# Gate and up products in three ranges of 375, 500 and 375 nodes, codes divided to match, and the feed-forward handed over by bank

## The reference, cut to what matters

```python
def act_qdq(x):                       # one scale for the whole array
    qmax = 2.0 ** (ACT_BITS - 1) - 1.0            # 32767
    scale = jnp.maximum(jnp.max(jnp.abs(x)) / qmax, 1e-12)
    return jnp.clip(jnp.round(x / scale), -qmax - 1.0, qmax) * scale
...
x = act_qdq(x)                                    # 1250 x 1024
up = act_qdq(x @ lpbq_dequant(w_up).T)            # 1250 x 384
gate = act_qdq(x @ lpbq_dequant(w_gate).T)
sig = fixed_qdq_u16(jax.nn.sigmoid(gate))
gate = act_qdq(gate * sig)
o = act_qdq(gate * up)
return o @ lpbq_dequant(w_down).T                 # 1250 x 1024
```

## Time and profile before

| what | us |
|---|---|
| median of 3 executions (1218.94 to 1221.99) | 1220.37 |
| the profiled execution | 1219.83 |
| its span, first to last instruction | 1218.0 |
| feed-forward products on PE, from 1074.17 to 1155.48 | 81.3 |
| handover, PE idle, 1155.48 to 1172.10 | 16.6 |
| down product on PE, from 1172.10 | 41.0 |

### The profile page before, as it was taken

The page is one execution under the profiler, slowest core; times in us unless marked ns, Lnnn a source line. Parts: engine busy times, 40 slices in busy tenths (PEclk is TensorE's granted clock), DMA queues, the critical chain, the costliest instruction groups (busy, mean ns, idle before and its releaser), DMA issues.

```text
span 1218.0 us, 15074 instructions
## 1 busy us (share of the span) xinstructions
PE 1150.2 (94%) x6232; PEld 617.6 (51%) x6232; DVE 680.2 (56%) x1225; ACT 355.0 (29%) x441; POOL 389.7 (32%) x224
## 2 busy tenths in 40 slices
PE   2998899999999999999999999999999999969958
PEld 2554455555555554444444555444444445559823
DVE  7769678656373584238434245746564355672663
ACT  5433333333333233322421122313110012253430
POOL 1267566768787675578100000000000000000000
PEclk9899899999999999999999999999999999989979
DMA  8843653352433437723730134323220080000014
GB/s 258 321 121 54 175 146 83 57 109 20 91 52 58 109 71 226 211 37 118 266 106 1 60 115 153 115 87 110 85 82 18 19 154 1 1 1 1 1 35 134
DMA packets 155997, 117.61 MB, mean 97 GB/s; under 512 B 93372, under 2 KB 132540, under 8 KB 154904
## 3 DMA queue, kind: packets, MB, share of 16 engines
q1 hardware_dynamic: 86616, 103.44, 27.0%
q0 software_dynamic: 69024, 13.07, 8.2%
q10 hardware_dynamic: 288, 0.13, 0.0%
HBM read 90.13 MB, written 21.41 MB: 92 GB/s over the span
## 4 chain that ended last, share of the span: by engine, by line
PE 88%; DVE 6%; issue 2%; ACT 2%; DMA 1%; POOL 0%; SPq 0%; POOLq 0%; ACTq 0%; DVEq 0%
PE ps L1011 34%; PE ps L943 27%; PE ps L1071 7%; PE ps L1043 7%; PE ps L1096 6%; PE ps L1116 3%; PE ps L930 2%; DVE key_b L1198 1%; DMA raw<-in_L_gnn_W_self_dram 1%; DVE whl L1180 1%; PE ps L1059 1%; PE ps L907 1%; PE ps L951 0%; DVE xnT L1186 0%; DVE T L1274 0%
## 5 line engine op out<-in xcount | busy, mean ns | idle before, releaser
L576 POOL DMA_INDIRECT at_scratch<-copies,cell x160 | 342.0, 2137 | 170.8 <-DMA at_scratch<-copies,cell 94.5
L943 PE MATMUL ps<-xnT,whl 128*128 128x512 f16 (+1 forms) x2160 | 385.8, 342 | 4.3 <-DVE T L1278 4.3
L943 PEld LDWEIGHTS ps<-xnT,whl 128*128 128x128 f16 x2160 | 211.8, 99 | 176.0 <-issue 8.9
L1011 PE MATMUL ps<-hb,hT 128*128 128x512 f16 x960 | 207.7, 379 | 1.3 <-DVE hT L1455 1.3
L1011 PEld LDWEIGHTS ps<-hb,hT 128*128 128x128 f16 x960 | 94.0, 98 | 114.4 <-DVE hT L1455 1.8
L1011 PE MATMUL ps<-hb,VT 128*128 128x512 f16 x480 | 103.9, 379 | 1.5 <-ACT S_b L718 1.5
L557 POOL PARTITION_ALL_REDUCE ag_fw<-am_fw x9 | 3.2, 355 | 317.0 <-DVE am_fw L1335 317.0
L1011 PE MATMUL ps<-hb,xnT 128*128 128x512 f16 x480 | 104.2, 379 | 0.0
L1071 PE MATMUL ps<-P,AT 125*128 125x512 f16 x400 | 87.8, 379 | 0.0
L1043 PE MATMUL ps<-AT,P 125*128 125x512 f16 (+1 forms) x480 | 84.7, 339 | 0.0
L1011 PEld LDWEIGHTS ps<-hb,VT 128*128 128x128 f16 x480 | 46.9, 98 | 58.0 <-ACT S_b L718 1.9
(11 more groups left out here) (218 smaller groups left out, 1164.0 us busy)
## 6 DMA issues: line engine op xcount, KB each, us to landing
raw<-in_L_gnn_W_neigh_dram SPq DMA_DIRECT2D x32, 512.0 KB
raw<-in_L_gnn_W_self_dram SPq DMA_DIRECT2D x24, 512.0 KB
key_b<-key_scratch SPq DMA_DIRECT2D x8, 1250.0 KB, 11.4
raw<-in_L_mix_Wo_dram SPq DMA_DIRECT2D x16, 512.0 KB
parts<-at_scratch POOLq DMA_DIRECT2D x20, 312.5 KB, 3.8
at_scratch<-zeros POOLq DMA_DIRECT2D x6, 1020.0 KB, 17.8
x_all<-in_x_dram SPq DMA_DIRECT2D x9, 512.0 KB
x_acc<-in_x_dram SPq DMA_DIRECT2D x9, 512.0 KB, 7.8
```

Of the source, the lines that this page charges most:

```text
L576: pool.indirect_dma_start(out=at_scr[c % 2][:, :], out_offset=bass.IndirectOffsetOnAxis(ap=cell[:, c:c + 1], axis=0), in_=copies[:, c:c + ...
L943: mm = pe.matmul(acc_of(c)[:, a:b], whl[:, i, wp, k, :], xnT[:, k, ap, a:b], start=(k == 0 and wp == 0 and ap == 0), stop=(k == KC - 1 and ...
L1011: mm = pe.matmul(half_bank(i), stationary[:, k, ap, t * TP:t * TP + P], hb[:, n % 2, k, wp, :], start=(k == 0 and wp == 0 and ap == 0), st ...
```

## The change

Five edits, all behind time 1066:

1. `FCOLS` becomes three ranges of 375, 500 and 375 nodes: six products of 72 matmuls each, with 375 or 500 columns, in place of ten with 250.
2. `PIECES` follows: range 0 is coded in pieces of 2, 3 and 3 feature chunks by 375 nodes, then come 250, 250, 250 and 125 nodes by 8 chunks. `CODED` says how many pieces a range needs. The last piece (tile 9 alone) comes on ACT behind `ug_out(0)`.
3. The up products 4 and 5 are copied out and their maxima taken behind the whole gate chain. The last product signals by bank (`ug_bank`), ACT copies bank by bank (`u_part`) and DVE takes each bank's maximum.
4. `TMP` and `TMP2` are computed by ACT, behind its rounding of `U` (`o_times`). The first chunk of `U` is cut at node 500 (`UPARTS`): DVE rounds 500 nodes itself, ACT the rest.
5. Nodes 0 to 124 of `o` are coded in two pieces, chunk 0 and chunks 1 and 2 (`OPIECES`), and PE starts the down product on the first.

```diff
-    FCOLS = [(a, a + 2 * TP) for a in range(0, N, 2 * TP)]
+    FCOLS = [(0, 3 * TP), (3 * TP, 7 * TP), (7 * TP, N)]
...
-    PIECES = [(0, 0, KC // 2), (0, KC // 2, KC)] + [(r, 0, KC) for r in range(1, NR_F)]
+    PIECES = [(0, 3 * TP, 0, 2), (0, 3 * TP, 2, 5), (0, 3 * TP, 5, KC)] + [
+        (a * TP, b * TP, 0, KC) for a, b in ((3, 5), (5, 7), (7, 9), (9, NT))]
+    CODED = [3, 5, 7]
...
+    OPIECES = [(0, 1, 0, TP), (1, IC, 0, TP)] + [(0, IC, a, b) for a, b in OCOLS[1:]]
+    OFIRST = 2
+    UPARTS = [slice(0, 4 * TP), slice(4 * TP, N)] + [slice(c * N, (c + 1) * N) for c in range(1, IC)]
...
+            for n in range(len(PIECES) - 1):
+                code_high(n)
+            turned_x2(NT - 1)
             act.wait_ge(s_ug_ok, 1)
-            for n in range(NR_F):
+            ug_out(0)
+            code_high(len(PIECES) - 1)
+            for n in range(1, NR_F):
                 ug_out(n)
...
+                    if n + 1 == len(UG):
+                        act.wait_ge(ug_bank, b + 1)
...
+            act.activation(sv[:, TMP2:TMP2 + 1], sv[:, Q_GS:Q_GS + 1], ACT.Copy,
+                           scale=sv[:, Q_U:Q_U + 1]).then_inc(o_times, 1)
...
-                    pe.wait_ge(c_lo, r + 2)
+                    pe.wait_ge(c_lo, CODED[r])
...
-                pe.wait_ge(o_lo, r + 1)
+                if r > 0:
+                    pe.wait_ge(o_lo, OFIRST + r)
...
+                            if i == 0 and k < OFIRST:
+                                pe.wait_ge(o_lo, k + 1)
...
-            ug_max(2 * NR_F - 2)
-            steps(ug_max(2 * NR_F - 1))
+            for n in range(NR_F, 2 * NR_F - 1):
+                ug_max(n)
+            for b in range(IC):
+                lo, hi = FCOLS[NR_F - 1]
+                dve.wait_ge(u_part, b + 1)
+                last = dve.tensor_reduce(omax[:, 0, IC * (NR_F - 1) + b:IC * (NR_F - 1) + b + 1],
+                                         U[:, b * N + lo:b * N + hi], AX.X, ALU.max, apply_absolute_value=True)
...
-            steps(dve.tensor_scalar(sv[:, TMP:TMP + 1], sv[:, Q_GS:Q_GS + 1], sv[:, Q_U:Q_U + 1], 1 / 65536.0,
-                                    ALU.mult, ALU.mult))
-            steps(dve.tensor_scalar(sv[:, TMP2:TMP2 + 1], sv[:, TMP:TMP + 1], 1 / 32767.0, None, ALU.mult))
```

More of the change, by code:

```diff
@@ L844, in _ @@
                     turned_x2(t)
[L847 to L851, removed]
             def ug_out(n):
@@ L877, in _ @@
                                scale=65536.0).then_inc(sig_ok, 1)
-                ug_out(NR_F + c)
+                if c == 1:
+                    ug_out(NR_F)
             act.wait_ge(gs_step, 1)
@@ L881, in _ @@
                 round_code(G[:, cols(c)], Q_GS, gs_round)
-            ug_out(2 * NR_F - 2)
-            ug_out(2 * NR_F - 1)
+            for n in range(NR_F + 1, 2 * NR_F):
+                ug_out(n)
             act.wait_ge(u_step, 1)
-            for c in range(1, IC):
-                round_code(U[:, cols(c)], Q_U, u_round)
+            for part in UPARTS[1:]:
+                round_code(U[:, part], Q_U, u_round)
+            act.activation(sv[:, TMP2:TMP2 + 1], sv[:, Q_GS:Q_GS + 1], ACT.Copy,
+                           scale=sv[:, Q_U:Q_U + 1]).then_inc(o_times, 1)
+            act.wait_ge(o_times, 1)
+            act.activation(sv[:, TMP:TMP + 1], sv[:, TMP2:TMP2 + 1], ACT.Copy, scale=1 / 65536.0).then_inc(o_times, 1)
+            act.wait_ge(o_times, 2)
+            act.activation(sv[:, TMP2:TMP2 + 1], sv[:, TMP:TMP + 1], ACT.Copy, scale=1 / 32767.0).then_inc(o_times, 1)
             act.wait_ge(o_step, 1)
-            for r, (a, b) in enumerate(OCOLS):
-                if r == 0:
-                    act.wait_ge(o_code, 1)
-                else:
[L892 to L895, removed]
+            for n, (k0, k1, a, b) in enumerate(OPIECES):
+                if n < OFIRST:
+                    act.wait_ge(o_code, n + 1)
+                else:
+                    act.activation(chunks(G)[:, k0:k1, a:b], chunks(G)[:, k0:k1, a:b], ACT.Identity,
+                                   bias=pos_magic[:, :], scale=sv[:, Q_O + 1:Q_O + 2]).then_inc(o_round, 1)
+                    act.wait_ge(o_round, n - OFIRST + 1)
+                act.activation(o16[:, k0:k1, 0, a:b], chunks(G)[:, k0:k1, a:b], ACT.Identity,
                                bias=neg_magic[:, :]).then_inc(o_hi, 1)
@@ L1092, in _ @@
                     for k in range(KC):
-                        if n == 0 and b == 0 and k % (KC // 2) == 0:
-                            pe.wait_ge(c_lo, k // (KC // 2) + 1)
+                        if n == 0 and b == 0 and k in FIRST_CODED:
+                            pe.wait_ge(c_lo, FIRST_CODED.index(k) + 1)
                         for wp, ap in ((0, 0), (0, 1), (1, 0)):
@@ L1619, in _ @@
                 steps(dve.tensor_scalar(G[:, cols(c)], G[:, cols(c)], MAGIC, None, ALU.subtract))
-            ug_max(2 * NR_F - 2)
-            steps(ug_max(2 * NR_F - 1))
-            code_step(MU, omax[:, 0, :], Q_U, 1.0, u_step)
-            steps(dve.tensor_scalar(sv[:, TMP:TMP + 1], sv[:, Q_GS:Q_GS + 1], sv[:, Q_U:Q_U + 1], 1 / 65536.0,
-                                    ALU.mult, ALU.mult))
-            steps(dve.tensor_scalar(sv[:, TMP2:TMP2 + 1], sv[:, TMP:TMP + 1], 1 / 32767.0, None, ALU.mult))
[L1626 to L1632, removed]
+            for n in range(NR_F, 2 * NR_F - 1):
[5 more added lines that the diff above has]
+                                         U[:, b * N + lo:b * N + hi], AX.X, ALU.max, apply_absolute_value=True)
+            steps(last)
+            code_step(MU, omax[:, 0, :], Q_U, 1.0, u_step)
+            for n, part in enumerate(UPARTS):
+                if n > 0:
+                    dve.wait_ge(u_round, n)
+                code(U[:, part], Q_U, rounded=n > 0)
+                steps(dve.scalar_tensor_tensor(G[:, part], U[:, part], MAGIC, G[:, part], ALU.subtract, ALU.mult))
+                last = dve.tensor_reduce(omax[:, 2, n:n + 1], G[:, part], AX.X, ALU.max, apply_absolute_value=True)
             steps(last)
-            whole_max(MO, omax[:, 2, 0:IC])
+            whole_max(MO, omax[:, 2, 0:len(UPARTS)])
+            dve.wait_ge(o_times, 3)
             steps(dve.tensor_scalar(sv[:, Q_O:Q_O + 1], ag[:, MO:MO + 1], sv[:, TMP2:TMP2 + 1], 1e-12,
@@ L1640, in _, with o_low @@
             dve.wait_ge(o_step, 1)
[L1642 to L1650, removed]
+            def o_low(n):
+                k0, k1, a, b = OPIECES[n]
+                dve.wait_ge(o_hi, n + 1)
+                dve.scalar_tensor_tensor(o16[:, k0:k1, 1, a:b], chunks(G)[:, k0:k1, a:b], MAGIC,
+                                         o16[:, k0:k1, 0, a:b], ALU.subtract, ALU.subtract).then_inc(o_lo, 1)
+            for k0, k1, a, b in OPIECES[:OFIRST]:
+                dve.tensor_scalar(chunks(G)[:, k0:k1, a:b], chunks(G)[:, k0:k1, a:b], sv[:, Q_O + 1:Q_O + 2], MAGIC,
+                                  ALU.mult, ALU.add).then_inc(o_code, 1)
+            o_low(0)
             steps(dve.tensor_scalar(sv[:, S_DN:S_DN + 1], i_fw[:, 0:1], sv[:, Q_O:Q_O + 1], None, ALU.mult))
-            for r in range(len(OCOLS)):
-                o_low(r)
+            for n in range(1, len(OPIECES)):
+                o_low(n)
             for i in range(2 * NT):
```

30 lines of the change are left out of this document (17 added, 13 removed).

## The result

| | before | after |
|---|---|---|
| median of 6 executions each, us | 1220.73 | 1214.33 (1213.7 to 1215.55) |
| ratio | | 0.9953, 95% interval 0.9943 to 0.9964 |
| a second comparison, on another occasion, us | 1220.57 | 1215.56, ratio 0.9957 (0.994 to 0.9973) |
| profiled execution, us | 1219.83 | 1214.49 |
| span, us | 1218.0 | 1212.7 |

What follows compares the result with a forecast made beforehand. TensorE, busy 94% of 1218.0 us, was taken to bound the kernel, with its waits. Seven terms (-0.98, -1.85, +0.11, -1.04, -0.44, -0.12, -0.68) sum to -5.00: 1220.37 to 1215.4 us, range 1213.5 to 1218.0.

Steps and rivals of the forecast that it cites:

- Matmuls: Gate and up products: 288 matmuls of 375 and 144 of 500 columns replace 720 of 250, 77.1 to 76.1 us, -0.98.
- Stall: PE's wait between product 1 and product 2, behind ACT's copy of product 0, goes away: -1.85 us.
- Start: First code pieces and product 0: PE starts 0.61 us earlier but loses 2.2 instead of 1.5 in product 0; together +0.11.
- Last range: Behind PE's last up product: one bank's copy and maximum, 1.15 us, replace three copies and a maximum, 2.19; -1.04.
- Scalar products: In the handover, two scalar products leave DVE's path and hide on ACT behind its rounding: -0.44 us.
- First piece of o: From the scale of o to PE's start of the down product: 1.99 us becomes 1.31, -0.68, bounds -0.3 and -0.9.
- First chunk of U: In the handover: scaling 500 instead of 1250 elements saves 0.39 us, one more product and maximum costs 0.26; -0.12.
- Clock: Both PE blocks start at 1.2 GHz; where the clock rises may move each block by 0.6 us either way.
- the clock held through product 0: Rival: clock stays at 1.2 GHz through product 0, +8.9 us, sum +3.9, 1224.3 us; chance 0.04.
- a clock held longer and small gains: Rival: small pieces don't pay or PE's gaps hold the clock down, 1.5 us; sum -2.7, 1217.7 us; chance 0.14.
- The odd starts: Rival: ranges 1 and 2 stream f16 from an odd element; 15% more per matmul gives 1223.4 us; chance 0.04.
- The two bank signals: Rival: all three copies and maxima still stand behind PE's end; sum -3.3, 1217.0 us; chance 0.04.

Runs made afterwards that it cites:

- e1: Kernel before, only ScalarE's order changed: product 0 copied out ahead of the last code piece, still five ranges of 250; 1217.76 us against 1219.47, ratio 0.9987.
- e8_two_pieces: Changed kernel with range 0 coded in two pieces of four feature chunks instead of three of 2, 3 and 3; executed once, 1216.27 us.
- e2: Changed kernel with the whole handover of before put back, leaving new ranges, code pieces and ScalarE's order; 1217.91 us, ratio 0.9984.
- e5: Changed kernel with the last up range handed over as one again (three copies, one maximum of 1125 values); executed once, 1215.78 us.
- after_again: The changed kernel run once more, unaltered, on another occasion; 1215.56 us, ratio 0.9957 to the kernel before.
- e9: Changed kernel plus 60 unused matmuls in the handover and 28 ahead of product 0; 1213.18 us, ratio 0.9942 to the kernel before.
- e10: As e9, with VectorE scaling the fourth code piece behind the third's low code instead of ahead of it; 1212.34 us, ratio 0.9934 to the kernel before.
- e3: Kernel before with the new handover alone (last up range by bank, scalar products on ScalarE, U cut, o in two pieces); 1216.89 us, ratio 0.998.
- e4_warm_handover: Changed kernel plus 60 unused matmuls of 512 columns between the last product and the down product; 1211.45 us against 1219.47 before, ratio 0.9932.

## Why the prediction was right

- **The sum.** Forecast -5.0 from the profiled execution, measured -5.3, but not by the same terms: the change itself, to the start of the down product, gave -4.65, where the terms said -5.0; the down product lost 0.61 to the clock; and 1.31 came from ahead of the change. So that -5.3 stands so near to -5.0 is in part luck: without the 1.31 the two profiles differ by 4.0. In these two profiles the place where the clock rose went against the change; by the estimate in the result that is about 0.3 of what -4.65 lacks, and the 0.61. The median fell to 1214.33, 1.1 below the forecast 1215.4.
- **Matmuls, -0.98.** Too large, by 0.35 over products 1 to 5 (65.03 us where my rates give 64.68) and by 0.43 if product 0 is counted at the same rates. Product 2, 72 matmuls of 375 columns, ran from 1101.92 to 1113.44: 0.1600 each and not 0.1589; the 144 of 500 take the rest of the 65.03, 0.2116 each and not 0.2108. The line between 250 and 512 columns was mis-sized. The 0.2116 also meets one of my signs of being wrong (over 0.211), at a price of some 0.1 us.
- **Stall, -1.85.** Right: no wait in 360 matmuls, and e1 shows that the order on ScalarE alone does it.
- **Start, +0.11.** PE started 2.69 behind the first scaling (2.68 by my working) and product 0 ended at 16.40 (16.34). Two small misses cancel in it: PE had piece 2 at 7.15 and not 7.28, and its 57 matmuls took 9.26 and not 9.06. Three rows of 375 took 995 ns in the kernel after, as charged (1.00) and not 0.87; in e8_two_pieces four rows took 998 ns, so three rows do cost what four do. The Trainium skill, "Vector Engine (DVE) Microarchitecture Reference", section 5.1, has the first port take the larger half of an odd outermost count, and these two rows agree with it.
- **Last range, -1.04.** Right in size (done 1.19 us behind PE's end, against 2.19). It hides two opposite effects that e2 and e5 part: +0.7 for the wider range, -1.7 for going by bank.
- **Scalar products, -0.44:** 0.44. **First piece of o, -0.68:** 0.66, and from the earlier trace rows's 1.99 to 1.25 in the changed kernel. **First chunk of U, -0.12:** the whole handover fell by 2.34 where these four terms said 2.28. U was not tried by itself, but from the first scaling of `U` to that of `o` it took 10.94 before (1159.17 to 1170.11) and 10.80 after (1154.09 to 1164.89): -0.14.
- **Clock.** Left out of the sum and put at 0.6 either way for each block. That was too narrow for both: product 0 ended 1.0 later in after_again and 1.2 later in e1 than in the runs of the same pieces beside them (12.50 before), and the down product lay between 40.59 and 42.00 with an idle handover, up to 1.0 above the 40.98 that I started from.
- **The rivals.** No run showed the clock held through product 0. Nor do PE's small gaps show as what holds it down: the rise came 3.4 to 6.1 us into product 0 with the three pieces, and 2.8, 3.2, 5.3 and 5.4 us with two pieces and no gap. The odd starts cost nothing that can be seen: product 0's last 24 matmuls (even start) were busy 3.99 us, product 2's (odd) 4.00. The two bank signals come apart in time, as the 0.58 and 0.56 of one bank behind the last matmul show. Of the rival with a clock held longer and small gains, the clock's part came in after_again, 1.0 us of its 1.5; the small gains did not (`o` 0.66, last range 1.00).
- **Open:** the 1.31 us ahead of the change. The code ahead of that point is the same in all fourteen kernels but for the 28 unused matmuls of e9 and e10, and yet the thirteen other profiles start their first scaling anywhere between 1068.95 and 1070.53, the one of before at 1070.88. Among them are e1 and e3, whose code ahead of it is that of before, at 1069.75 and 1069.64. That speaks for chance of that one execution; with one profile of before it isn't shown.

## What to carry to other kernels

Look for short work that stands in an engine's row behind long work and frees a buffer: moving one copy ahead of code pieces removed a stall of 1.85 us here, with no change of tiling. Going by bank at a hand-over between engines is worth more the wider the last range is, so a coarser tiling and a hand-over by bank belong together. Where the matrix engine waits several microseconds for a scale over the whole array, matmuls that nobody reads can keep its clock up: here 60 of them brought the down product from 40.6 to 42.0 us to 39.05, at no cost to the handover of 14.28.

## What the runs showed of the hardware

- The granted clock rose 2.8 to 6.1 us after PE took up work, in runs of the same code too (after: 3.4 us into product 0; after_again: 6.1). So the down product behind an idle handover took 1.5 to 3.0 us more than with the clock up (40.59 to 42.00, against 39.05), and where in that one execution falls no run ties to the code.
- Idle times of 0.80, 0.94 and 1.35 us left the clock at 1.00 (e9_warm_both in product 0, e4_warm_handover ahead of the down product); behind 2.34 us it was at 0.50.
- A matmul of 375 columns came every 160.0 ns and one of 500 every 211.6, so 3.8 and 3.3 ns above columns / 2.4 GHz, where 512 columns show 2.5 and 250 columns 2.9.
- An f32 scaling of three rows of 375 on VectorE took 995 ns, one of four such rows 998 (e8_two_pieces), and one of 1000 elements in eight rows of 125 took 741.
